# A cross-attention and feed-forward layer on one core: GpSimd's sums, VectorE's order and the spreading of a one-hot rearranged

## What is computed

```python
x = x + xattn(layernorm(x), ctx, ctx, mask, ...)      # 16 query heads of 16, one shared key/value head of 16, 64 keys
x = x + ffn(layernorm(x), ...)

# xattn: q = query @ Wq + bq; k = key @ Wk + bk; v = value @ Wv + bv
#        attn = softmax(where(mask == 0, -1e9, q k / 4)); return (attn v) @ Wo + bo
# ffn, with P = 9 paths of width 64:
x_mixed = mix_kernel[0]*x[s-1] + mix_kernel[1]*x[s] + mix_kernel[2]*x[s+1]
h = einsum('bsd,pdm->bspm', x_mixed, W1) + b1
stacked_paths = einsum('bspm,pmd->bspd', h, W2) + b2
scores = tanh(x_mixed @ Wo1 + bo1) @ Wo2 + bo2
weights = one_hot(argmax(scores), P)
collapsed = einsum('bspd,bsp->bsd', stacked_paths, weights)
return layernorm(x + collapsed) * gamma + beta
```

## Time and profile before

| | us |
|---|---|
| median of 3 runs (lowest, highest) | 396.97 (395.99, 398.92) |
| profiled execution | 397.85 |
| its span, first to last instruction | 396.0 |
| TensorE busy in the span (2764 products) | 335.4, 85% |
| VectorE busy | 265.0, 67% |
| GpSimd busy | 190.0, 48% |
| ScalarE busy | 182.7, 46% |

### The profile page before, as it was taken

How to read it: one execution, slowest core, us unless ns; L and a number is a source line. 1 busy time by engine, 2 the same in 40 slices (tenths; PEclk the granted TensorE clock), 3 DMA queues, 4 the chain that set the end, 5 groups by cost and what they waited for, 6 DMA issues and landing times.

```text
span 396.0 us, 7447 instructions
## 1 busy us (share of the span) xinstructions
PE 335.4 (85%) x2764; PEld 245.9 (62%) x2764; DVE 265.0 (67%) x590; ACT 182.7 (46%) x285; POOL 190.0 (48%) x225
## 2 busy tenths in 40 slices
PE   1686884894999999898999999899999799979990
PEld 0563472373467956686577856685678376966890
DVE  2346296278177846897399638885678754698866
ACT  1432744435445456435645454445651555357400
POOL 0240106201807349562939277744954496339234
PEclk9998995898899999999999999999999999999996
DMA  8308000100020001200120003000100010001003
GB/s 218 129 0 196 27 2 14 54 0 2 0 68 3 0 2 55 66 2 0 53 66 0 0 13 104 2 0 2 55 0 2 0 55 2 0 2 54 2 2 106
DMA packets 20421, 13.46 MB, mean 34 GB/s; under 512 B 10081, under 2 KB 20138, under 8 KB 20394
## 3 DMA queue, kind: packets, MB, share of 16 engines
q1 hardware_dynamic: 18754, 12.53, 10.8%
q10 hardware_dynamic: 1640, 0.57, 0.6%
HBM read 8.90 MB, written 4.19 MB: 33 GB/s over the span
## 4 chain that ended last, share of the span: by engine, by line
PE 44%; DVE 21%; POOL 11%; issue 9%; ACT 8%; DMA 5%; ACTq 1%; DVEq 0%; POOLq 0%; SPq 0%
PE ps L419 8%; DVE mx L1085 5%; PE ps L527 3%; PE ps L572 3%; PE ps L424 3%; DVE st L1032 3%; ACT xh L848 3%; DMA xin<-in_x 3%; PE ps L637 3%; PE ps L562 3%; POOL x L1391 3%; POOL x1b L1397 3%; DVE osb L1103 2%; DVE x L1111 2%; PE ps L553 2%
## 5 line engine op out<-in xcount | busy, mean ns | idle before, releaser
L1371 POOL TENSOR_TENSOR rs<-ve,halfneg 128x4 f32<-128x4 f32 x24 | 25.1, 1046 | 148.8 <-DVE ve L1048 148.8
L823 ACT ACTIVATE e<-ps 128x1024 f32<-128x1024 f32 x32 | 31.1, 1023 | 35.8 <-PE ps L534 35.8
L1079 DVE CAST qr<-q 128x512 fp32r<-128x512 f32 x16 | 8.6, 540 | 47.8 <-ACT q L811 47.4
L1085 DVE TENSOR_REDUCE mx<-ps 128x16 f32<-128x1024 f32 x32 | 37.7, 1210 | 0.7 <-PE ps L502 0.7
L655 PE MATMUL ps<-w2h,hmh 128*128 128x256 f32 (+1 forms) x140 | 35.8, 291 | 0.0
L656 PE MATMUL ps<-w2l,hmh 128*128 128x256 f32 (+1 forms) x140 | 34.6, 282 | 0.0
L419 PE MATMUL ps<-xmh,w1h 128*128 128x512 f32 x80 | 27.5, 425 | 6.2 <-ACT hs L874 4.0
L572 PE MATMUL ps<-wo,osb 128*128 128x256 f32 x128 | 31.3, 390 | 1.6 <-DVE osb L1103 1.6
L874 ACT ACTIVATE hs<-ps,b1s 128x512 f32<-128x512 f32 x28 | 19.4, 692 | 25.5 <-PE ps L424 25.5
L1428 POOL TENSOR_TENSOR hml<-hs,hmh 128x512 fp32r<-128x512 f32 x24 | 29.9, 1271 | 1.5 <-ACT hmh L884 1.5
L1417 POOL TENSOR_TENSOR y<-xh2f,gms 128x256 f32<-128x256 f32 x28 | 21.0, 781 | 20.1 <-DVE xh2f L1057 20.1
(11 more groups left out here) (155 smaller groups left out, 825.0 us busy)
## 6 DMA issues: line engine op xcount, KB each, us to landing
xin<-in_x SPq DMA_DIRECT2D x8, 512.0 KB, 3.7
out<-y SPq DMA_DIRECT2D x7, 512.0 KB, 2.9
min_<-in_mask_Bx1xSxS_ik SPq DMA_DIRECT2D x8, 128.0 KB, 3.6
cst<-in_constants SPq DMA_DIRECT2D x1, 660.5 KB, 10.0
hs<-in_L_ffn_W SPq DMA_DIRECT2D x2, 288.0 KB
hs<-in_L_ffn_W SPq DMA_DIRECT2D x1, 512.0 KB
out<-xin SPq DMA_DIRECT2D x2, 256.0 KB, 2.2
cst<-in_constants SPq DMA_DIRECT2D x1, 384.0 KB, 6.5
```

Of the source, the lines that this page charges most:

```text
L823: nc.scalar.activation(e[:, 2 * i:2 * i + 2, :], ps[:, bank:bank + 2, :], ACT.Exp).then_inc(s_e, 1)
L1085: v.tensor_reduce(mx[:, k, :].rearrange("p (a h) -> p a h", a=2), ps[:, bank:bank + 2, :].rearrange("p a (h s) -> p a h s", s=SK), AX.X, A ...
```

## The change

GpSimd: add_beta and add_bo leave the step's start. After the selected low parts comes `add_beta(next_f)` of the block whose feed-forward is next, then rstd2, then `add_bo(front)`, a step ahead of its use; x1b has two buffers for it. VectorE: `layernorm1_stats(after)` and the mix come first in a step with a feed-forward, ahead of q_round. TensorE: w1(0) and w1(4) move ahead of the second half of the scores and of wq; the one-hot is transposed once into PSUM (four 10-row transposes), ScalarE copies it to `ohT`, and each rep(m) is one product of a constant 10-row 0/1 matrix with ohT, 512 columns wide; rep(0) comes behind spread. ScalarE: exponentials in two halves with hidden(0) and hidden(4) between; the mixed high part and layernorm 1 ahead of pv_copy. Neither the block of SyncE nor its order is in the diff. The constants grow by 320 columns (and one of padding).

```diff
@@ buffers and constants
-C_N = C_IO + NPATH
+C_R = C_IO + NPATH + 1
+C_N = C_R + NM * P // 2
...
+    path = np.where(col < 4 * P + DM, col // DM, col - 4 * P - DM)
+    c[:, C_R:C_R + NM * P // 2] = as_bf16((r == path) & (r < NPATH))
...
-        x1b = sb("x1b", [P, NT, D])
+        ohT = thT[0:16, 0:CH // 2].bitcast(BF16)
+        x1b = sb("x1b", [P, NJ, NT, D])
...
-        NFA, NFV, NU = NM, NM + 3, 2 * NM + 3
+        NFA, NFV, NU = NM + 1, NM + 3, 2 * NM + 4
@@ TensorE
+            def onehot_transposed(b, j, L=usual):
+                o = take_slot(b, j, "ohT", L)[0:NPATH + 1, 0:CH // 2].bitcast(BF16)
+                pe.wait_ge(s_oh, at(b, NJ, j + 1))
+                for k in range(NT):
+                    mm = nc.tensor.transpose(o[:, k * P:(k + 1) * P], oh[:, k, :], ident_b[:, :])
+                mm.then_inc(L.s_f, 1)
+
             def rep(b, j, m, L=usual):
                 o = take_slot(b, j, f"rep{m}", L)
                 if m == 0:
-                    pe.wait_ge(s_oh, at(b, NJ, j + 1))
-                for k in range(NT):
-                    ...
-                mm.then_inc(L.s_f, 1)
+                    pe.wait_ge(L.s_fa, L.read_by_act(b, j, NFA))
+                r = rows_of(m)
+                nc.tensor.matmul(o[0:r, :], path_rows[0:NPATH + 1, m * P:m * P + r], ohT[0:NPATH + 1, :],
+                                 start=True, stop=True).then_inc(L.s_f, 1)
@@ TensorE, step
                 if n:
                     scores_transposed(*n, 0, front)
+                if f:
+                    w1(*f, 0)
+                    w1(*f, 4)
+                    scores_transposed(*n, 1, front)
                 if front:
                     wq(*front, fb)
-                if n:
+                if n and not f:
                     scores_transposed(*n, 1, front)
                 if f:
-                    w1(*f, 0)
-                    w1(*f, 4)
                     w1(*f, 1)
                     gate(*f)
...
                     w1(*f, 3)
-                    rep(*f, 0)
+                    onehot_transposed(*f)
...
                 if n:
                     spread(*n)
                 if f:
+                    rep(*f, 0)
                     rep(*f, 1)
@@ TensorE, tail
+            onehot_transposed(*f0)
+            w1(*f1, 4, last)
             rep(*f0, 0)
             rep(*f0, 1)
-            w1(*f1, 4, last)
...
+            onehot_transposed(*f1, last)
@@ ScalarE
+            def onehot_copy(b, j, L=usual):
+                act.wait_ge(L.s_f, L.filled(b, j, "ohT"))
+                nc.scalar.activation(ohT[0:NPATH + 1, :], ps[0:NPATH + 1, L.bank(j, "ohT"), 0:CH // 2].bitcast(BF16),
+                                     ACT.Copy).then_inc(L.s_fa, 1)
@@ ScalarE, step
                 if n:
-                    softmax_exp(*n)
+                    softmax_exp(*n, 0)
+                if f:
+                    hidden(*f, 0)
+                    hidden(*f, 4)
+                if n:
+                    softmax_exp(*n, 1)
                 if front:
                     q_copy(*front, 0 if f else 6)
                 if f:
-                    hidden(*f, 0)
-                    hidden(*f, 4)
-                if f:
                     hidden(*f, 1)
-                if n:
-                    pv_copy(*n)
-                if f:
-                    hidden(*f, 2)
-                    hidden(*f, 3)
                 if f and f[1] == 0:
                     mixed_hi(f[0], 1)
                 if f and n[1] == NJ - 1:
                     early_mixed_hi(n[0])
-                if f:
+                if after and f:
+                    layernorm1_apply(*after)
+                if n:
+                    pv_copy(*n)
+                if f:
+                    hidden(*f, 2)
+                    hidden(*f, 3)
+                    onehot_copy(*f)
                     keep_xh2(*f)
@@ VectorE, last_column: the wait for s_earlyl stands one instruction earlier
@@ VectorE, step
                 if after and not f:
                     layernorm1_stats(*after)
-                if front:
-                    q_round(*front)
+                if after and f:
+                    layernorm1_stats(*after)
                 if f and f[1] == 0:
                     second_mix(f[0])
                 if f and n[1] == NJ - 1:
                     early_mix(n[0])
+                if front:
+                    q_round(*front)
                 if f:
                     argmax(*f)
                 if n:
                     invert(*n)
-                if after and f:
-                    layernorm1_stats(*after)
@@ GpSimd
             def add_beta(b, j):
-                pool.wait_ge(s_yo, 1 + at(b, NJ, j))
+                pool.wait_ge(s_yo, at(b, NJ, j))
...
-            def step(n, front, f, after):
-                if f:
-                    add_beta(*f)
-                if n:
-                    add_bo(*n, f)
+            def step(n, front, f, after, next_f):
...
                 if f:
                     for m in range(NM):
                         selected_lo(*f, m)
+                if next_f:
+                    add_beta(*next_f)
                 if n:
                     rstd2(*n)
+                if front:
+                    if not next_f:
+                        pool.wait_ge(s_wo_in, 32)
+                    add_bo(*front, next_f)
```

More of the change, by code:

```diff
@@ L280, in layer_program @@
         class Usual(Path):
-            uses = ["h0", "h4", "h1", "gate", "h2", "h3", "rep0", "rep1", "rep2", "rep3", "rep4", "w2a", "w2b"]
-            by_act = [u in ("h4", "h0", "h1", "h2", "h3") for u in uses]
+            uses = ["h0", "h4", "h1", "gate", "h2", "h3", "ohT", "rep0", "rep1", "rep2", "rep3", "rep4", "w2a", "w2b"]
+            by_act = [u in ("h4", "h0", "h1", "h2", "h3", "ohT") for u in uses]
             first = 1
@@ L591, in take_slot @@
                     elif use[:3] == "rep":
-                        pe.wait_ge(L.s_fa, min(int(use[3]) + 2, NFA))
+                        pe.wait_ge(L.s_fa, min(int(use[3]) + 2, NM))
                     elif use == "w2a":
@@ L629, in rep @@
                 if m == 0:
-                    pe.wait_ge(s_oh, at(b, NJ, j + 1))
-                for k in range(NT):
[L632 to L639, removed]
-                                                  start=True, stop=True)
-                mm.then_inc(L.s_f, 1)
+                    pe.wait_ge(L.s_fa, L.read_by_act(b, j, NFA))
+                r = rows_of(m)
+                nc.tensor.matmul(o[0:r, :], path_rows[0:NPATH + 1, m * P:m * P + r], ohT[0:NPATH + 1, :],
+                                 start=True, stop=True).then_inc(L.s_f, 1)
             def w2_product(b, j, k, terms, L=usual):
@@ L674, in step @@
                     scores_transposed(*n, 0, front)
-                if front:
-                    wq(*front, fb)
-                if n:
-                    scores_transposed(*n, 1, front)
                 if f:
@@ L681, in step @@
                     w1(*f, 4)
+                    scores_transposed(*n, 1, front)
+                if front:
+                    wq(*front, fb)
+                if n and not f:
+                    scores_transposed(*n, 1, front)
+                if f:
                     w1(*f, 1)
@@ L816, in maxima, with softmax_exp @@
                 nc.scalar.activation(nmT[:, :], bf16_bank(bank), ACT.Copy).then_inc(s_nT, 1)
-            def softmax_exp(b, j):
+            def softmax_exp(b, j, half):
                 act.wait_ge(s_dn, at(b, NJ, j))
-                for i in range(4):
+                for i in (2 * half, 2 * half + 1):
                     act.wait_ge(s_st, at(b, NJ * NPAIR, j * NPAIR + 2 * i + 2))
@@ L891, in step @@
                 if f:
-                    hidden(*f, 0)
-                    hidden(*f, 4)
-                if f:
                     hidden(*f, 1)
+                if f and f[1] == 0:
+                    mixed_hi(f[0], 1)
+                if f and n[1] == NJ - 1:
+                    early_mixed_hi(n[0])
+                if after and f:
+                    layernorm1_apply(*after)
                 if n:
@@ L900, in step @@
                     hidden(*f, 3)
-                if f and f[1] == 0:
-                    mixed_hi(f[0], 1)
-                if f and n[1] == NJ - 1:
-                    early_mixed_hi(n[0])
-                if f:
+                    onehot_copy(*f)
                     keep_xh2(*f)
-                if f:
                     for m in range(NM):
                         selected_hi(*f, m)
-                if after:
+                if after and not f:
                     layernorm1_apply(*after)
@@ L949, in _ @@
             hidden(*f0, 3)
+            onehot_copy(*f0)
             keep_xh2(*f0)
+            hidden(*f1, 4, last)
             selected_hi(*f0, 0)
-            hidden(*f1, 4, last)
             selected_hi(*f0, 1)
@@ L960, in _ @@
             hidden(*f1, 3, last)
+            onehot_copy(*f1, last)
             for m in range(NM):
```

35 lines of the change are left out of this document (18 added, 17 removed).

## The result

The changed kernel takes 437.13 us (median of 4 runs, 435.58 to 440.37), against 396.94 before: ratio 1.1016, 95% interval 1.0941 to 1.1091. The forecast of 418.0 with its range of 409 to 427 has the sign and the place right, and is 19 us short. The profiled execution took 440.37 us, its span 438.5. Medians in this document are over all runs of a kernel, ratios over its fast runs alone.

A forecast was written before the change was run, and what follows sets the result against it. TensorE bound the kernel before; afterwards store, load, statistics, mix, rounding, pv. Profiled 397.85 + 25.0 - 0.2 - 1.2 - 2.0 - 0.7 = 418.95, with the median 0.9 below: 418.0 us, range 409 to 427.

The forecast's parts named there:

- steps 3 to 5: Passes n = 3 to 5, each beside block n-2's feed-forward; load behind store delays pv: 153.5 us against 128.46, +25.0.
- the stop: TensorE before pv in steps 3 to 5, waiting for q's rounding behind the late load: 9.6 us.
- step 2: Pass n = 2, whose load has no store ahead and comes early: -0.2 us.
- step 6: Pass n = 6, without a layernorm 1 of a later block: earlier pv, osb and rep4, -1.2 us.
- step 7 and tail: Last pass, W1 filling the wait for exponentials, -2.0 us; tail after it, rep4's wait gone, -0.7 us.
- step 3: Pass n = 3, beside block 1's feed-forward: 51.2 to 51.3 us long, against 43.34 before.
- 0.5 for products at the lower clock after the stop: pv's narrow products on TensorE, taken as bound by their issue: 0.5 us lost to the clock per stop.
- Rival 2: TensorE's clock falls in full after each of three stops, 2.6 us against 0.5 counted: 424 us; chance 0.15.
- I take 0.5: Input load directly behind a store: 0.5 us extra on top of 3.7, between bounds of nothing and 2.9.
- in a hole of 4.69 us before rstd2 ... so it is hidden: GpSimd's add_beta, 2.8 to 3.5 us, fits the hole before rstd2, hidden by at least 1 us.
- The one-hot products as cheaper, and nothing else: TensorE's one-hot products in each feed-forward: 2.66 us become 1.45, 1.2 saved, mostly off the path.
- Rival 1: The intended gain: load in SBUF when VectorE frees, needing it to pass the store: 388 us; chance 0.08.

The follow-up runs named there:

- e4: The changed kernel with 36 unused products of 512 columns on TensorE between the wait for q and the wait for the rounded q; 447.3 us (one run).
- e14: Changed kernel, loads before store, statistics behind invert, 64-row one-hot products, add_beta behind layernorm 2's roots, add_bo behind layernorm 3's; 394.91 us.
- e15: The kernel of e14 with GpSimd's order of the changed kernel (add_beta beside split_max); 398.06 us, ratio 1.0005.
- e16: The kernel of e14 with GpSimd's two lower halves of the mixed columns ahead of add_beta and add_bo in step 2 alone; 390.19 us.
- e8: The kernel of e3 with 128-row operands, both from the constants, in each one-hot product (selection by path left out); 397.49 us, ratio 1.0001.
- e3: The kernel before with the one-hot change alone, products of ten rows; 403.8 us, ratio 1.0171.
- e13: The changed kernel with one-hot products over 64 rows instead of ten, the added rows zero; 433.74 us, ratio 1.0884.
- e1: The changed kernel with SyncE's input load of the block after next issued ahead of the store; 402.96 us, ratio 1.0127.
- e12: The kernel of e1 with 64-row one-hot products, add_beta moved behind rstd2 and add_bo behind finish; 438.67 us.
- e10: The kernel before with the mix in front of q's rounding alone, and the TensorE and ScalarE order belonging to it; 403.14 us, ratio 1.0143.

## Why the prediction was wrong

The mechanism held in each point that it named: store and load back to back in steps 3 to 5 and only there, VectorE standing for the load, pv held behind the cast of q, no stop in steps 2 and 6. Store and load were 0.7 to 1.0 us apart, where 0.4 was forecast. The working has a slip of 0.2: its own terms add up to 418.75 for the profiled execution, where it writes 418.95. Measured are 440.37, and the missing 21.6 us are terms that were mis-sized or put at nothing. The largest in the stop itself is the price of the low clock behind it: 0.5 us in the sum, 2.4 to 2.8 us measured.

| | predicted | measured |
|---|---|---|
| steps 3 to 5 | +25.0 | +36.9 |
| step 2 | -0.2 | +2.0 |
| step 6 | -1.2 | +0.3 |
| step 7 and tail | -2.7 | +1.8 |
| up to step 2 | 0 | +1.6 |

In step 3 (+7.9 predicted, +12.5 measured) they can be read one by one:
- **"0.5 for products at the lower clock after the stop"**, because pv's products were called "bound by their issue". They were not: 3.64 us against 1.92 at half the clock. From pv to osb it took 12.77 us (168.53 to 181.30) instead of 10.35, so 2.4 more. e4 shows the cause. Rival 2 had the mechanism, with 2.6 us; it belonged in the forecast.
- **"I take 0.5"** for a load behind a store, on top of 3.7: 5.09 us were measured where 4.2 was taken, 0.9 more, and the load was issued 0.3 us later in the step. Statistics, mix and rounding took 0.1 less together, so pv came 23.0 us into the step instead of 22.0: 1.0 more. In steps 4 and 5 the wait was 4.00 and 4.85 us, so this term was too small in steps 3 and 5 and not in step 4.
- **add_beta "in a hole of 4.69 us before rstd2 ... so it is hidden"**. It was hidden on GpSimd. But the hole lies beside VectorE's split_max, which takes 1.3 us longer for it, and osb to the transposes took 17.46 us instead of 16.2. e14 and e15 show 1.34 us in each of steps 3 to 6. It is also why step 6 gained nothing: without it -1.2 was nearly right (39.33 in e16 against 40.38 before). The Trainium skill (GPSIMD Engine Reference, Key points) says that GpSimd shares its SBUF interfaces with VectorE and contends with instructions of two SBUF inputs or in a two-port mode. A cast at 1.21 instead of 0.29 us and a difference of two SBUF tiles at 0.84 instead of 0.43 agree with it (the difference has two SBUF inputs; in which mode the cast runs no trace shows); the prediction had used this effect for the mix (3.9 or 6.3 us) and not for what it moved itself.

These make 4.7 us, for a gap of 4.6 in step 3.

**The one-hot products as cheaper, and nothing else:** this is the term that failed outside the stop. In themselves they are: with 128 rows (e8) steps 3 to 5 are 42.41, 41.62 and 42.14 us, 2.3 less than before in the three, and e3's with ten rows are about the same (42.38, 41.70 and 42.17). As ten-row products they cost the clock, 6.3 us by e3 against e8 and 3.4 by the changed kernel against e13. In the profiled executions e13 is 4.6 us shorter in step 2, step 7 and the tail, of the 6.7 us by which these came out worse than forecast. That the clock could fall where TensorE waits no longer than 0.84 us was on no list of mine.

The 1.6 us up to step 2 can't be put down to the change: the kernels with the one-hot change begin that step between 96.9 and 101.1 us, those with the old products between 98.1 and 100.0.

Rival 1, the gain (388), said what it would need: the load past the store. With the load first e1 had that and still took 403, for the two prices that the rival didn't have either, clock and split_max. With both mostly paid off, and with the statistics back behind invert, which the rival did not have, e16 stands at 390.2.

## What to carry to other kernels

When work moves to where its input is early, follow every condition of that input on the queue that issues it: this load had two, its place behind a store and a sum on GpSimd, and either alone, with the statistics in front, made a step 12 us longer. "Hidden" has to be shown for both engines: the one that does the work, and the one whose instructions run beside it. And an operand of few rows made a product that took as long as a full one, with slower ones behind it: rows filled up with zeros took no longer (0.38 to 0.39 us) and won 3.4 us here, though in two profiled executions the clock fell behind them all the same.

## What the runs showed of the hardware that was not expected

- Three bf16 products of ten rows and 512 columns ahead of a projection, with waits of no more than 0.84 us beside them, and the granted clock falls to 0.53 (e3) and 0.54 (changed kernel, step 2) for the projection (3.5 to 3.7 us for 2.0). With 128 rows, or with 64 of which 54 are zero, no projection of eight in the profiled executions was slow, but two W1 products behind 64-row ones were (e14 and e12, 1.22 and 1.21 us instead of 0.73).
- pv's products of 512 columns into 32 outputs and the denominators' of 128 columns follow the clock: 3.60 us together at full, 6.44 us with the clock at 0.50 and then 0.61.
- VectorE's cast of 256 f32 elements a partition to bf16 takes 0.29 us alone and 1.22 beside a GpSimd sum, four times as long, while the GpSimd sum takes 2.87 instead of 2.81 us. Beside VectorE's mix it is GpSimd that slows: 3.98 instead of 2.81 us for y (e10).
